# Sparse experts behind a shared one: a longer lag between the two products, weights in smaller parts, other orders of loads

## The chip, the cores and the metric
One NeuronCore of one Trainium2 chip. The metric is the device time of one execution in microseconds, median of the runs; lower is better. Everything is float32: each product of two float32 matrices is made of three matmuls, high x high, high x low and low x high, of the parts into which the operands are split.

## The reference, cut to what matters
x is [4, 1024, 512], so 4096 tokens of 512 features.

```
x = x + ((x * ys) @ weight) * d                         # modulated linear, ys and d from cond
s = sigmoid(concat(x, cond) @ router_W)                 # 8 experts
pick 2 experts of (s + router_bias) per token, gates = s_sel / sum(s_sel)
shared = (silu(x @ w1) * (x @ w3)) @ w2                 # 512 -> 1024 -> 512
routed = sum over the 2 experts: gate * (gelu(x @ W1e[e]) @ W2e[e])   # 512 -> 512 -> 512
out = x + (shared + routed) / 3
```

The router's weights are scaled up and its bias is drawn with a wide spread, so the load of the experts is uneven. From the inputs, 8192 (token, expert) rows fall on experts 4, 5, 6 and 7 alone: 3160, 622, 314 and 4096.

## The kernel before
Tokens go in 8 blocks of 512 (NBLK) through the linear layer and the router, then again in 8 blocks through the shared network, each in 8 chunks of 128 hidden features (HC): `up(n, hc, j)` is 24 matmuls, `down(n, hc)` 12. Meanwhile SP, ACT and DVE split the experts' weights into high and low parts, piece by piece (`move_piece`, `piece_high`, `piece_low`: load eraw, split into ehl, store to we_d), and POOL sorts the tokens by expert in memory: `put_row` scatters the rows of x1 with their token number and gate into xs_d.

Then come the experts. xs_d is cut into 71 tiles of 128 rows (TILES, the most that any routing needs), each of one expert; rows and tiles that the routing leaves empty are padding with gate 0 and a token number beyond the last token, one of 128 extra rows of out (PADROWS). Such rows are written by the loop at L1151. Per tile t:
- SP (pairs 0 and 1) or POOL (`load_pair`, L1170) loads x rows into xg, DVE turns them (`turn_x`), ACT and DVE split them (`x_high_of`, `take_x`).
- TensorE: `matmul1(t)`, 12 matmuls; ACT: gelu (`hidden`), and four DMAs hid to hturn (`move_h`, L676); DVE: `turn_h`; ACT, DVE: split (`h_high_of`, `take_h`).
- TensorE: `matmul2(t)`, 12 matmuls; DVE scales the result by the gate into ys (`take_y`, L1078); POOL adds it to the rows of out by an indirect DMA (`scatter`, L1184).

The loops run in a fixed order on each engine. TensorE's is matmul1(t), matmul2(t - LAG), with LAG = 3; ACT and DVE turn h of tile t - TURN_LAG, with TURN_LAG = 2. hid, hturn and ys have 4 buffers (RING), the split operands and the banks 2. So ys of tile t waits for the add of tile t - 4. An add waits for the one two tiles back; it also waits for the one just before unless both tiles are of one expert and neither is an unused tile (`scatter_waits` makes the table: `same`, `tail`).

Expert weights sit in four places (WRING) of 32 KB per partition, each in two halves, W1e and W2e, of 2 MB over all partitions. The used experts are numbered by turn. SP loads halves 0 to 7 for turns 0 to 3 first. Half 0 is loaded during block 6 of the shared network; half 1 waits for the last `up`, because place 0's second half and places 1 to 3 lie over w13h, w13l, the split w2 and xl. After that come the last store of out (`store_out(NBLK - 1)`, L282) and halves 2 to 7 (L328), each waited for before the next. Then, for rounds r = 4 to 7, SP reads a table, waits until TensorE has finished the tiles of turn r - 4 (L377; unused rounds all wait for the same tile, the last of turn 0) and loads two halves in four parts of 512 KB each (`load_in_parts`, L334), waiting for each part before it issues the next. This is done whether an expert is used or not. SP ends with waits for all stores and adds.

POOL, once the rows are sorted, waits for the scatter table and for the last store of out, then asks for pairs 2 and 3 of x, and then runs over the tiles: every second tile one more pair, and one scatter per tile.

Of the kernel before, what the change touches and what calls it, by code (L numbers as in the profile page):

```python
# [7 lines left out]
FP32 = mybir.dt.float32  # L8
FP32R = mybir.dt.float32r
INT32 = mybir.dt.int32  # L10
# [20 lines left out]
PAIR = 2  # L31
PADDED = -(-TILES // PAIR) * PAIR
SLOTS = PADDED * P
TURN_LAG = 2
LAG = TURN_LAG + 1
PADROWS = P
Q = 32
PADS = (SLOTS - K * TOK) // P
ROW = D + 2
XB = 4  # L40
EPS = 1e-8
# [24 lines left out]
def shared_moe_kernel(nc, xT, w0, condT, router_w, router_b, shared_w, expert_w, consts, tokid, padslots, padrows, out):  # L66
# [8 lines left out]
    with ctx:  # L75
        base = -(-nc.sbuf_base // 128) * 128

        def sb(name, shape, dt, kib):
            return nc.alloc_sbuf_tensor_at(name, [P] + shape, dt, offset=base + int(kib * KIB))

        def sem(name):
            return ctx.enter_context(nc.semaphore(name))


        x1t = sb("x1t", [2, DC, BLK], FP32, 0)
        w13h = sb("w13h", [HC, 2, DC, P], FP32R, 16)
        w13l = sb("w13l", [HC, 2, DC, P], FP32R, 48)
        wmh = sb("wmh", [2, DC, D], FP32R, 80)
        wml = sb("wml", [2, DC, D], FP32R, 96)
        w2h = wmh[:, :, :, :].rearrange("p b c n -> p (b c) n")  # L90
# [18 lines left out]
        xgt = sb("xgt", [2, DC, P], FP32, 192)  # L109
        wait_for = sb("wait_for", [TILES], INT32, 196)  # L110
        same = sb("same", [TILES], INT32, 196.5)
        tail = sb("tail", [TILES], INT32, 197)
        x1tok = sb("x1tok", [BLK // Q, DC, Q], FP32, 168)
        w0sq = sb("w0sq", [DC, D], FP32, 160)
        xres = sb("xres", [SUB, D], FP32, 160)
# [12 lines left out]
        def small(name, shape, dt=FP32):  # L128
            n = 1
            for s in shape:  # L130
                n *= s
            t = sb(name, shape, dt, at[0])
            at[0] += -(-n * 4 // 32) * 32 / KIB
            assert base + at[0] * KIB <= nc.sbuf_usable_end
            return t
# [15 lines left out]
        rec = small("rec", [K, NT, 2], INT32)  # L151
        sadr = small("sadr", [K, NT], INT32)
        padr = small("padr", [PADS], INT32)
        pad = small("pad", [3, 2 * E])
        slot = small("slot", [PADDED, 2], INT32)

# [57 lines left out]
        weights_in = sem("weights_in")  # L214
        xrow_in = [sem(f"xrow_in{b}") for b in range(XB)]
        xrow_out = [sem(f"xrow_out{b}") for b in range(XB)]
        rec_put, pad_done, zero_in, pad_out = sem("rec_put"), sem("pad_done"), sem("zero_in"), sem("pad_out")
        xg_in = [sem(f"xg_in{j}") for j in range(2)]
        xg_soft = [sem(f"xg_soft{j}") for j in range(2)]
        xturn_done, hturn_done, mm1_done, mm2_done = sem("xturn_done"), sem("hturn_done"), sem("mm1_done"), sem("mm2_done")  # L220
# [11 lines left out]
        def _(sp):  # L232
# [11 lines left out]
            sp.dma_start(xin[:, 1], xT[1]).then_inc(xin_in[1], 16)  # L244
            for j in range(2):
                sp.dma_start(wraw[:, j, :], shared_w[j]).then_inc(wraw_in[j], 16)
            sp.dma_start(out[TOK:TOK + PADROWS, :], padrows).then_inc(pads_in, 16)

            for n in range(NBLK):

# [57 lines left out]
            for n in range(NBLK - 2):  # L308
                for hc in range(HC):
                    if piece_at(n, hc):  # L310
                        move_piece(n, hc)
                    if n == 0 and hc == 1:
                        store_x1(0)
                    if n == 0 and hc == 2:
                        load_res(0)
                    if n and hc == 1:
                        store_out(n - 1)
                        load_res(n)
                    if hc == 5:
                        store_x1(n + 1)  # L320
                        load_x1t(n, n % 2)
# [4 lines left out]
            def load_weight(i, e, place):  # L326

                sp.dma_start(we[:, place, i % 2].rearrange("p a h s c n -> p (a h) (s c n)").bitcast(FP32),  # L328
                             we_d[bass.ds(e * 4 + i % 2 * 2, 2)].rearrange("h p s n -> p h (s n)").bitcast(FP32)).then_inc(we_in[i % HRING], 16)

            def load_in_parts(i, e, place):

                for q in range(4):
                    sp.dma_start(we[:, bass.ds(place, 1), i % 2, q // 2, q % 2].rearrange("p a c n -> p (a c n)").bitcast(FP32),  # L334
                                 we_d[bass.ds(e * 4 + i % 2 * 2 + q // 2, 1), :, q % 2].rearrange("a p n -> p (a n)").bitcast(FP32)).then_inc(we_in[i % HRING], 16)
                    sp.wait_ge(we_in[i % HRING], 16 + 16 * (q + 1))
                sp.sem_inc(weights_in, 1)

            def weight_loaded(i):
# [23 lines left out]
            for j in range(SUB):  # L363
                sp.dma_start(slot[j * Q:(j + 1) * Q], xs_rec[j]).then_inc(slots_in, 16)

            sp.wait_ge(ab_done, HC * NBLK)
            load_weight(1, first[0], slice(0, 1))
            store_out(NBLK - 1)
            weight_loaded(1)


            for i in range(2, HRING):
                load_weight(i, first[i // 2], slice(i // 2, i // 2 + 1))
                weight_loaded(i)
            for r in range(WRING, E):
                e, place, over = table(0, r, E - 1), table(1, r, WRING - 1), table(2, r, TILES)
                sp.wait_ge(mm2_done, over + 1)  # L377
                for i in (2 * r, 2 * r + 1):
                    load_in_parts(i, e, place)
            sp.wait_ge(pads_in, 16)  # L380
            sp.wait_ge(out_stored, 16 * NBLK)
            for j in range(2):
                sp.wait_ge(added[j], 16 * ((TILES - j + 1) // 2))
# [3 lines left out]
        def _(pe):  # L387
# [69 lines left out]
            def up(n, hc, j):  # L457

                q = HC * n + hc
                if hc == 0:  # L460
                    pe.wait_ge(xl_ready, 4 * (NBLK + n + 1))
                pe.wait_ge(gm_done, q + 1)
                for ps, m in ((a_ps, 0), (b_ps, 1)):
                    for c in range(DC):
                        w_hi, w_lo = w13h[:, hc, m, c, :], w13l[:, hc, m, c, :]
                        pe.matmul(ps[hc % 2][:, :], w_hi, xh[:, j, c, :], start=(c == 0), stop=False)  # L466
                        pe.matmul(ps[hc % 2][:, :], w_hi, xl[:, j, c, :], start=False, stop=False)  # L467
                        last = pe.matmul(ps[hc % 2][:, :], w_lo, xh[:, j, c, :], start=False, stop=(c == DC - 1))  # L468
                last.then_inc(ab_done, 1)
# [100 lines left out]
        def _(act):  # L570
# [13 lines left out]
            for n in range(NBLK):  # L584

                act.wait_ge(xin_in[(n + 1) % 2], 16 * ((n + 1) // 2) + 16)
                act.wait_ge(lin_done, DC * n + 1)
                for c in range(DC):
                    x_high((n + 1) % 2, c, mod[:, c, (n + 1) // 2:(n + 1) // 2 + 1] if n + 1 < NBLK else 1.0)
                if n == 0:  # L590
                    act.wait_ge(prep, 4)
                    act.activation(dtmp[:, :, :], dvar[:, :, :], ACT.Sqrt).then_inc(root, 1)

                act.wait_ge(wraw_in[n % 2], 16 * (n // 2) + 16)
                act.activation(w13h[:, n].rearrange("p m c n -> p (m c n)"), wraw[:, n % 2, :], ACT.Copy).then_inc(w_high, 1)

            def w2_high(g):

# [102 lines left out]
        def _(dve):  # L701
# [49 lines left out]
            for n in range(NBLK):  # L751
# [13 lines left out]
                        else:  # L765
                            x_low(n + 1, (n + 1) % 2, c)
                dve.wait_ge(w_high, n + 1)
                w_hi = w13h[:, n].rearrange("p m c n -> p (m c n)").bitcast(FP32)
                dve.tensor_tensor(w13l[:, n].rearrange("p m c n -> p (m c n)"), wraw[:, j, :], w_hi, ALU.subtract).then_inc(w_split, 1)

            def w2_low(g):
                dve.wait_ge(w_high, HC + g + 1)
# [130 lines left out]
            def pad_rows():  # L903
# [18 lines left out]
                then(dve.tensor_tensor(grid, grid, begin[:, 0:E + 1].unsqueeze(1).to_broadcast([P, PADS, E + 1]), ALU.mult))  # L922
                then(dve.tensor_reduce(dst[:, 0:PADS], grid, AX.X, ALU.max))
                then(dve.tensor_tensor(dst[:, 0:PADS], dst[:, 0:PADS], place, ALU.add))
                dve.tensor_copy(padr[:, :], dst[:, 0:PADS]).then_inc(pad_done, 1)

            def slot_rows():
# [151 lines left out]

            def scatter_waits():  # L1080

                at, used = cst[0:1, C_TIX:C_TIX + TILES], e8[0:1, 1, E - 1:E]
                then(dve.tensor_scalar(wait_for[0:1, :], at, 1.0, None, ALU.add))
                then(dve.tensor_scalar(wait_for[0:1, :], wait_for[0:1, :], 1, 255, ALU.logical_shift_right, ALU.bitwise_and))
                then(dve.tensor_tensor(same[0:1, 1:TILES], turn_of[0:1, 1:TILES], turn_of[0:1, 0:TILES - 1], ALU.is_equal))
                then(dve.tensor_scalar(tail[0:1, :], at, used, None, ALU.is_lt))
                then(dve.tensor_tensor(same[0:1, 1:TILES], same[0:1, 1:TILES], tail[0:1, 1:TILES], ALU.mult))
                then(dve.tensor_tensor(same[0:1, 1:TILES], wait_for[0:1, 1:TILES], same[0:1, 1:TILES], ALU.subtract))
                dve.tensor_scalar(wait_for[0:1, 1:TILES], same[0:1, 1:TILES], 16.0, None, ALU.mult).then_inc(waits_done, 1)

# [20 lines left out]
        def _(pool):  # L1111
# [28 lines left out]
            pool.wait_ge(tables_done, 3)  # L1140
            pool.wait_ge(sadr_done, K)
            pool.wait_ge(pad_done, 1)
            pool.dma_start(xrow[:, XB - 1, 0:D], padrows).then_inc(zero_in, 16)
            pool.dma_start(xrow[:, XB - 1, D:ROW].bitcast(INT32), padslots[:, 0:2]).then_inc(zero_in, 16)
            for i in range(XB - 1):
                load_row(i)
# [1 line left out]
            for g in range(PADS):  # L1148
                if g:
                    pool.wait_ge(pad_out, 16 * g)  # L1150
                pool.indirect_dma_start(xs_d[:, :], IO(padr[:, g:g + 1], 0), xrow[:, XB - 1, :], None).then_inc(pad_out, 16)  # L1151
            pool.wait_ge(pad_out, 16 * PADS)
            load_row(XB - 1)
            for i in range(0, NT, 2):
# [3 lines left out]
                for m in (i, i + 1):  # L1158
                    if m + XB < NT:
                        row_free(m)  # L1160
                        load_row(m + XB)
            pool.wait_ge(waits_done, 1)

            def load_pair(m):

# [18 lines left out]
                pool.indirect_dma_start(out[:, :], IO(slot[:, t, 0:1], 0), ys[:, t % RING, :], None,  # L1184
                                        compute_op=ALU.add).then_inc(added[t % 2], 16)

            pool.wait_ge(out_stored, 16 * NBLK)
            load_pair(2)
            load_pair(3)
            for t in range(TILES):  # L1190
                if t % 2 == 0:
                    load_pair(t // 2 + 4)
                scatter(t)
# [56 lines left out]
```

## Time and profile before
| | us |
|---|---|
| median of 3 runs (1078.06 to 1082.4) | 1079.09 |
| profiled execution, device time | 1082.94 |
| its span | 1081.1 |
| TensorE busy | 1030.0 |
| DVE busy | 507.4 |
| POOL busy | 332.3 |
| ACT busy | 292.7 |

The page's busy times are of the span of the profiled execution. The span falls into the linear layer (to about 116 us), the shared network (to about 647), and the experts. The engines' rows in the 40 slices show TensorE at 9 tenths or more in all but the first, one in the middle and the last few; the DMA engines' share is at 9 tenths or more in most slices of the experts' stage. A wait row names who ended the wait, by the last event that the profile shows.

### The profile page before, as it was taken

Reading aid. Unit: us, or ns where it says so; the run is one execution under the profiler, and the core shown is the slowest. Engines: PE = TensorE matmul, PEld = TensorE weight load, DVE = VectorE, ACT = ScalarE, POOL = GpSimd, SP = SyncE. Lnnn points to the kernel's source line nnn. Section 1 sums busy time; section 2 is a strip of 40 time slices with the busy share of each in tenths; the row PEclk is TensorE's granted clock in tenths of the full one; section 3 lists DMA queues with packets and bytes.
Section 4 is the critical chain, followed back from the end, with each engine's and each line's share of the span. In section 5 each row is a group of like instructions: output and inputs, shape, how many; then the busy total and the mean of one; then the engine's idle time right before and its main releaser. Section 6 shows DMA issues by size and latency. Waiting matters only on the chain.

```text
span 1081.1 us, 14559 instructions
## 1 busy us (share of the span) xinstructions
PE 1030.0 (95%) x4692; PEld 841.7 (78%) x4692; DVE 507.4 (47%) x829; ACT 292.7 (27%) x461; POOL 332.3 (31%) x385
## 2 busy tenths in 40 slices
PE   6999999999999999999999995989999999999993
PEld 5888778887888888888888883878888887878782
DVE  4565456577324324324232123555555555555452
ACT  3222252332222222222111122223333333233230
POOL 1000000001113424334324102445545555555532
PEclk9999999999999999999999998999999999999997
DMA  5566587768867676877735629997779999999963
GB/s 177 195 216 228 205 285 258 243 242 237 280 217 263 209 271 225 244 276 238 235 96 155 134 78 282 294 266 136 155 135 197 238 200 230 219 223 213 210 126 56
DMA packets 132026, 226.77 MB, mean 210 GB/s; under 512 B 28848, under 2 KB 83760, under 8 KB 122864
## 3 DMA queue, kind: packets, MB, share of 16 engines
q1 hardware_dynamic: 59168, 142.22, 40.9%
q0 software_dynamic: 31328, 64.11, 26.2%
q10 hardware_dynamic: 41472, 19.68, 8.2%
q8 instruction: 35, 0.57, 0.2%
q14 instruction: 23, 0.19, 0.1%
HBM read 111.01 MB, written 96.54 MB: 192 GB/s over the span
## 4 chain that ended last, share of the span: by engine, by line
PE 75%; DMA 16%; DVE 3%; issue 3%; ACT 1%; SPq 1%; POOLq 0%; POOL 0%; DVEq 0%
DMA we<-we_d 12%; PE banks L466 10%; PE banks L467 10%; PE banks L468 10%; PE banks L528 7%; PE banks L530 7%; PE banks L529 7%; PE banks L480 5%; PE banks L481 5%; PE banks L482 5%; DMA out<-ys,slot 4%; PE banks L414 3%; PE banks L415 3%; PE banks L416 3%; PE banks L446 1%
## 5 line engine op out<-in xcount | busy, mean ns | idle before, releaser
L466 PE MATMUL banks<-xh,w13h 128*128 128x512 f32 x512 | 200.1, 391 | 1.8 <-DVE xl L723 1.8
L468 PE MATMUL banks<-xh,w13l 128*128 128x512 f32 x512 | 199.9, 390 | 0.0
L467 PE MATMUL banks<-xl,w13h 128*128 128x512 f32 x512 | 199.9, 390 | 0.0
L1184 POOL DMA_INDIRECT out<-ys,slot x71 | 123.9, 1745 | 202.5 <-DMA out<-ys,slot 118.8
L791 DVE SCALAR_TENSOR_TENSOR gm<-sil,banks 128x512 f32<-128x512 f32 x64 | 43.9, 687 | 248.2 <-ACT sil L609 248.2
L528 PE MATMUL banks<-we,hidth 128*128 x284 | 114.3, 402 | 16.2 <-issue 15.2
L1071 DVE TENSOR_TENSOR hidtl<-hidt,hidth 128x512 fp32r<-128x512 f32 x71 | 49.2, 693 | 161.6 <-ACT hidth L683 161.6
L609 ACT ACTIVATE sil<-banks 128x512 f32<-128x512 f32 x64 | 38.3, 598 | 314.8 <-PE banks L468 314.8
L1170 POOL DMA_DIRECT2D xg<-xs_d x136 | 99.9, 1113 | 63.1 <-DMA out<-outst 51.0
L528 PE MATMUL banks<-we,xgth 128*128 x284 | 111.4, 392 | 5.0 <-issue 4.4
L466 PEld LDWEIGHTS banks<-xh,w13h 128*128 128x128 f32 x512 | 96.7, 189 | 22.4 <-issue 2.3
L530 PE MATMUL banks<-we,hidtl 128*128 x284 | 112.4, 396 | 0.0
L529 PE MATMUL banks<-we,hidth 128*128 x284 | 112.2, 395 | 0.0
L468 PEld LDWEIGHTS banks<-xh,w13l 128*128 128x128 f32 x512 | 96.5, 188 | 20.2
L467 PEld LDWEIGHTS banks<-xl,w13h 128*128 128x128 f32 x512 | 96.5, 188 | 19.9
L529 PE MATMUL banks<-we,xgth 128*128 x284 | 110.6, 389 | 0.0
L530 PE MATMUL banks<-we,xgtl 128*128 x284 | 110.5, 389 | 0.0
L683 ACT ACTIVATE hidth<-hidt 128x512 fp32r<-128x512 f32 x71 | 44.9, 633 | 215.3 <-PE banks L530 126.7
L480 PE MATMUL banks<-wmh,gh 128*128 128x512 f32 x256 | 100.5, 392 | 2.5 <-DVE gl L795 1.9
L481 PE MATMUL banks<-wml,gh 128*128 128x512 f32 x256 | 100.4, 392 | 0.0
L482 PE MATMUL banks<-wmh,gl 128*128 128x512 f32 x256 | 100.3, 392 | 0.0
L528 PEld LDWEIGHTS banks<-we,hidth 128*128 128x128 f32 x284 | 54.1, 190 | 35.1 <-issue 24.2
(163 smaller groups left out, 1465.0 us busy)
## 6 DMA issues: line engine op xcount, KB each, us to landing
we_d<-ehl SPq DMA_DIRECT2D x32, 1024.0 KB, 6.4
hturn<-hid ACTq DMA_DIRECT2D x284, 64.0 KB
xg<-xs_d POOLq DMA_DIRECT2D x136, 128.0 KB
eraw<-expert_w SPq DMA_DIRECT2D x32, 512.0 KB, 5.0
we<-we_d SPq DMA_DIRECT2D x8, 2048.0 KB, 10.3
we<-we_d SPq DMA_DIRECT2D x32, 512.0 KB, 6.2
x1t_d<-x1t SPq DMA_DIRECT2D x8, 1024.0 KB, 8.6
xin<-x1t_d SPq DMA_DIRECT2D x8, 1024.0 KB, 9.4
```

Source lines behind the costliest of these rows:

```text
L466: pe.matmul(ps[hc % 2][:, :], w_hi, xh[:, j, c, :], start=(c == 0), stop=False)
L467: pe.matmul(ps[hc % 2][:, :], w_hi, xl[:, j, c, :], start=False, stop=False)
L468: last = pe.matmul(ps[hc % 2][:, :], w_lo, xh[:, j, c, :], start=False, stop=(c == DC - 1))
L480: pe.matmul(o_ps[s][:, :], g_hi, w2h[:, hc, :], start=(hc == 0), stop=False)
L481: pe.matmul(o_ps[s][:, :], g_hi, w2l[:, hc, :], start=False, stop=False)
L482: last = pe.matmul(o_ps[s][:, :], g_lo, w2h[:, hc, :], start=False, stop=(hc == HC - 1))
L528: pe.matmul(ps, high[:, c, :], w_hi, start=(c == 0), stop=False)
L529: pe.matmul(ps, high[:, c, :], w_lo, start=False, stop=False)
L530: last = pe.matmul(ps, low[:, c, :], w_hi, start=False, stop=(c == DC - 1))
L1071: dve.tensor_tensor(hidtl[:, t % 2], hidt[:, t % 2], hidth[:, t % 2].bitcast(FP32), ALU.subtract).then_inc(hidt_done, 1)
L1170: pool.dma_start(xg[g * Q:(g + 1) * Q, m % 2 * PAIR:(m % 2 + 1) * PAIR].rearrange("p t a n -> p (t a) n"), xs_d[m * PAIR * P:(m + 1) * PAI ...
L1184: pool.indirect_dma_start(out[:, :], IO(slot[:, t, 0:1], 0), ys[:, t % RING, :], None, compute_op=ALU.add).then_inc(added[t % 2], 16)
```

## The change: lag, parts, order of loads, padding
- TURN_LAG 3 and LAG 4, so matmul2 runs four tiles behind matmul1.
- w13h and w13l become one tensor w13 with high and low parts of a chunk side by side, so that 16 KB become free with every two chunks. Halves 1 to 3 of the experts' weights wait for `ab_done` of the last block's chunks (2, 4 and 6 done), not for the whole block.
- Half 4 waits for the last `up` and is loaded in parts, then `store_out(NBLK - 1)` is issued, and then halves 5 to 7, also in parts. A part is 256 KB, 8 to a half, in rows of 2 KB, each waited for before the next.
- POOL asks for pairs 2 and 3 of x before it waits for the last store of out.
- Padding rows have their own row of out, 8 x 128 of them (PADROWS); POOL writes the token numbers of each pad group by one more copy. The zeros for them (2 MB) are stored in block 1 of the shared network instead of 256 KB at the start. Unused tiles of one turn no longer wait for the add just before (`tail` goes).

```
-TURN_LAG = 2
+TURN_LAG = 3
 LAG = TURN_LAG + 1
-PADROWS = P
+PADROWS = PADS * P
...
-        w13h = sb("w13h", [HC, 2, DC, P], FP32R, 16)
-        w13l = sb("w13l", [HC, 2, DC, P], FP32R, 48)
+        w13 = sb("w13", [HC, 2, 2 * DC * P], FP32R, 16)
...
-            sp.dma_start(out[TOK:TOK + PADROWS, :], padrows).then_inc(pads_in, 16)
...
+                    if n == 1 and hc == 3:
+                        sp.dma_start(out[TOK:TOK + PADROWS, :], padrows).then_inc(pads_in, 16)
...
+            parts_before = [16 if i < 4 else 0 for i in range(HRING)]
+
             def load_in_parts(i, e, place):
 
-                for q in range(4):
-                    sp.dma_start(we[:, bass.ds(place, 1), i % 2, q // 2, q % 2].rearrange("p a c n -> p (a c n)").bitcast(FP32),
-                                 we_d[bass.ds(e * 4 + i % 2 * 2 + q // 2, 1), :, q % 2].rearrange("a p n -> p (a n)").bitcast(FP32)).then_inc(we_in[i % HRING], 16)
-                    sp.wait_ge(we_in[i % HRING], 16 + 16 * (q + 1))
+                for q in range(8):
+                    half, part, c = q // 4, q // 2 % 2, q % 2
+                    sp.dma_start(we[:, place, i % 2, half, part, c].rearrange("p a n -> p (a n)").bitcast(FP32),
+                                 we_d[bass.ds(e * 4 + i % 2 * 2 + half, 1), :, part, c * D:(c + 1) * D].rearrange("a p n -> p (a n)").bitcast(FP32)).then_inc(we_in[i], 16)
+                    sp.wait_ge(we_in[i], parts_before[i] + 16 * (q + 1))
+                parts_before[i] += 128
                 sp.sem_inc(weights_in, 1)
...
-            sp.wait_ge(ab_done, HC * NBLK)
-            load_weight(1, first[0], slice(0, 1))
-            store_out(NBLK - 1)
-            weight_loaded(1)
-
-
-            for i in range(2, HRING):
+            for i in (1, 2, 3):
+                sp.wait_ge(ab_done, HC * (NBLK - 1) + 2 * i)
                 load_weight(i, first[i // 2], slice(i // 2, i // 2 + 1))
                 weight_loaded(i)
+            sp.wait_ge(ab_done, HC * NBLK)
+            load_in_parts(4, first[2], slice(2, 3))
+            store_out(NBLK - 1)
+            for i in range(5, HRING):
+                load_in_parts(i, first[i // 2], slice(i // 2, i // 2 + 1))
             for r in range(WRING, E):
                 e, place, over = table(0, r, E - 1), table(1, r, WRING - 1), table(2, r, TILES)
                 sp.wait_ge(mm2_done, over + 1)
                 for i in (2 * r, 2 * r + 1):
-                    load_in_parts(i, e, place)
-            sp.wait_ge(pads_in, 16)
+                    load_in_parts(i % HRING, e, bass.ds(place, 1))
...
+                then(dve.tensor_scalar(padtok[:, :], tid[:, 0:PADS], float(TOK), None, ALU.add))
...
-                then(dve.tensor_scalar(tail[0:1, :], at, used, None, ALU.is_lt))
-                then(dve.tensor_tensor(same[0:1, 1:TILES], same[0:1, 1:TILES], tail[0:1, 1:TILES], ALU.mult))
...
+                pool.tensor_copy(xrow[:, XB - 1, D:D + 1].bitcast(INT32), padtok[:, g:g + 1]).then_inc(pad_put, 1)
+                pool.wait_ge(pad_put, g + 1)
                 pool.indirect_dma_start(xs_d[:, :], IO(padr[:, g:g + 1], 0), xrow[:, XB - 1, :], None).then_inc(pad_out, 16)
...
-            pool.wait_ge(waits_done, 1)
...
-            pool.wait_ge(out_stored, 16 * NBLK)
             load_pair(2)
             load_pair(3)
+            pool.wait_ge(waits_done, 1)
+            pool.wait_ge(pads_in, 16)
+            pool.wait_ge(out_stored, 16 * NBLK)
```

## Rows read from the trace of the kernel before
**Rows 1.** The page, part 1: busy us (share of span) x instructions.
```profile
PE 1030.0 (95%) x4692; PEld 841.7 (78%) x4692; DVE 507.4 (47%) x829; ACT 292.7 (27%) x461; POOL 332.3 (31%) x385
```
**Rows 2.** Windows of 5 us: us, busy by engine, granted clock, DMA share, GB/s.
```profile
670.00:675.00 5.00, 4.20 (x10) 3.33 (x11) 2.88 (x5) 2.00 (x4) 2.30 (x4) 0.50 1.03 351
```
**Rows 3.** TensorE's timeline: start us, us, engine, line, what [idle before <-releaser].
```profile
646.88 0.39 PE L528 MATMUL banks<-we,xgth 128*128 x1
...
660.86 0.49 PE L528 MATMUL banks<-we,xgth 128*128 x1 [1.68 <-issue]
...
670.80 0.79 PE L528 MATMUL banks<-we,hidth 128*128 x1 [6.39 <-issue]
...
962.79 0.39 PE L528 MATMUL banks<-we,xgth 128*128 x1
...
968.23 0.39 PE L528 MATMUL banks<-we,xgth 128*128 x1
```
**Rows 4.** Timelines of DVE, ACT's queue and POOL, 640 to 740 us.
```profile
665.38 0.71 DVE L1052 STREAM_TRANSPOSE xgt<-xg 128x512 f32<-128x512 f32 x1 [4.72 <-DMA xg<-xs_d]
668.50 0.71 DVE L1065 STREAM_TRANSPOSE hidt<-hturn 128x512 f32<-128x512 f32 x1 [2.42 <-DMA hturn<-hid]
...
650.48 3.53 ACTq L676 DMA_DIRECT2D hturn<-hid  x4
...
655.38 4.70 POOL L1170 DMA_DIRECT2D xg<-xs_d  x8 [50.96 <-DMA out<-outst]
```
**Rows 5.** Timelines of DVE and POOL at the end.
```profile
1065.68 0.75 DVE L1078 TENSOR_SCALAR ys<-banks,slot 128x512 f32<-128x512 f32 x1 [2.52 <-PE banks L530]
...
1047.29 1.55 POOL L1184 DMA_INDIRECT out<-ys,slot  x1 [4.17 <-DMA out<-ys,slot]
...
1075.77 1.55 POOL L1184 DMA_INDIRECT out<-ys,slot  x1 [4.50 <-issue]
```
**Rows 6.** SP's timeline from 540 us: start, us from first to last issue, what.
```profile
610.97 5.81 SPq L364 DMA_DIRECT2D slot<-xs_d  x4
641.38 0.42 SPq L328 DMA_DIRECT2D we<-we_d  x1
649.59 0.40 SPq L282 DMA_DIRECT2D out<-outst  x1
...
812.16 211.97 SPq L334 DMA_DIRECT2D we<-we_d  x32
```
**Rows 7.** POOL: a copy of its timeline, and a wait (us, times, longest).
```profile
602.63 0.54 POOL L1129 COPY xrow<-rec 128x2 int32<-128x2 int32 x1
...
POOL xrow L1119 <- DMA x_d<-x1tok: 17.5, 1, 17.5
```
**Rows 8.** Timelines of SP and ACT in block 1 of the shared network.
```profile
230.53 0.33 SPq L304 DMA_DIRECT2D eraw<-expert_w  x1
...
240.57 0.60 ACT L609 ACTIVATE sil<-banks 128x512 f32<-128x512 f32 x1 [5.23 <-PE banks L468]
```
**Rows 9.** Landing times of L328 (2048 KB), then of L334 (512 KB).
```profile
DMA to landing us min/median/max: 7.7/10.3/13.8
...
DMA to landing us min/median/max: 4.5/6.2/9.8
```
**Rows 10.** SP's waits, 812 to 1024 us: us, times, longest.
```profile
SPq L334 <- DMA we<-we_d: 142.6, 24, 9.2
...
SPq L337 <- DMA we<-we_d: 45.3, 7, 9.4
```
**Rows 11.** Landing of other DMAs: 200 to 500 us; SP's loads of xg.
```profile
x_d<-x1tok SPq DMA_DIRECT2D x19, 256.0 KB, 5.8
...
xg<-xs_d SPq DMA_DIRECT2D x8, 128.0 KB, 3.2
```
**Rows 12.** DMA queues, 812 to 1024 us: packets, MB, share of 16 engines.
```profile
q0 software_dynamic: 9111, 19.92, 48.4%
...
q10 hardware_dynamic: 21590, 9.83, 21.5%
```

More of the change, by code:

```diff
@@ L111, in shared_moe_kernel @@
         same = sb("same", [TILES], INT32, 196.5)
-        tail = sb("tail", [TILES], INT32, 197)
         x1tok = sb("x1tok", [BLK // Q, DC, Q], FP32, 168)
@@ L153, in shared_moe_kernel @@
         padr = small("padr", [PADS], INT32)
+        padtok = small("padtok", [PADS], INT32)
         pad = small("pad", [3, 2 * E])
@@ L216, in shared_moe_kernel @@
         xrow_out = [sem(f"xrow_out{b}") for b in range(XB)]
-        rec_put, pad_done, zero_in, pad_out = sem("rec_put"), sem("pad_done"), sem("zero_in"), sem("pad_out")
+        rec_put, pad_put, pad_done, zero_in, pad_out = sem("rec_put"), sem("pad_put"), sem("pad_done"), sem("zero_in"), sem("pad_out")
         xg_in = [sem(f"xg_in{j}") for j in range(2)]
@@ L464, in up @@
                     for c in range(DC):
-                        w_hi, w_lo = w13h[:, hc, m, c, :], w13l[:, hc, m, c, :]
+                        w_hi, w_lo = (w13[:, hc, k, (m * DC + c) * P:(m * DC + c + 1) * P] for k in range(2))
                         pe.matmul(ps[hc % 2][:, :], w_hi, xh[:, j, c, :], start=(c == 0), stop=False)
@@ L594, in _ @@
                 act.wait_ge(wraw_in[n % 2], 16 * (n // 2) + 16)
-                act.activation(w13h[:, n].rearrange("p m c n -> p (m c n)"), wraw[:, n % 2, :], ACT.Copy).then_inc(w_high, 1)
+                act.activation(w13[:, n, 0, :], wraw[:, n % 2, :], ACT.Copy).then_inc(w_high, 1)
             def w2_high(g):
@@ L767, in _ @@
                 dve.wait_ge(w_high, n + 1)
-                w_hi = w13h[:, n].rearrange("p m c n -> p (m c n)").bitcast(FP32)
-                dve.tensor_tensor(w13l[:, n].rearrange("p m c n -> p (m c n)"), wraw[:, j, :], w_hi, ALU.subtract).then_inc(w_split, 1)
+                dve.tensor_tensor(w13[:, n, 1, :], wraw[:, j, :], w13[:, n, 0, :].bitcast(FP32), ALU.subtract).then_inc(w_split, 1)
             def w2_low(g):
@@ L1080, in scatter_waits @@
             def scatter_waits():
-                at, used = cst[0:1, C_TIX:C_TIX + TILES], e8[0:1, 1, E - 1:E]
-                then(dve.tensor_scalar(wait_for[0:1, :], at, 1.0, None, ALU.add))
+                then(dve.tensor_scalar(wait_for[0:1, :], cst[0:1, C_TIX:C_TIX + TILES], 1.0, None, ALU.add))
                 then(dve.tensor_scalar(wait_for[0:1, :], wait_for[0:1, :], 1, 255, ALU.logical_shift_right, ALU.bitwise_and))
                 then(dve.tensor_tensor(same[0:1, 1:TILES], turn_of[0:1, 1:TILES], turn_of[0:1, 0:TILES - 1], ALU.is_equal))
-                then(dve.tensor_scalar(tail[0:1, :], at, used, None, ALU.is_lt))
-                then(dve.tensor_tensor(same[0:1, 1:TILES], same[0:1, 1:TILES], tail[0:1, 1:TILES], ALU.mult))
                 then(dve.tensor_tensor(same[0:1, 1:TILES], wait_for[0:1, 1:TILES], same[0:1, 1:TILES], ALU.subtract))
@@ L1142, in _ @@
             pool.wait_ge(pad_done, 1)
-            pool.dma_start(xrow[:, XB - 1, 0:D], padrows).then_inc(zero_in, 16)
+            pool.dma_start(xrow[:, XB - 1, 0:D], padrows[0:P]).then_inc(zero_in, 16)
             pool.dma_start(xrow[:, XB - 1, D:ROW].bitcast(INT32), padslots[:, 0:2]).then_inc(zero_in, 16)
```

## The prediction
> **What bounds the kernel now.** I read the page first: TensorE is busy 95% of the span [rows 1], so two questions follow: where it stands still, and what comes after its last instruction. The windows of 5 us put one weak place in front: 670 to 675 runs at a granted clock of 0.50, so at 1.2 GHz and not 2.4, with 10 matmuls [rows 2]. TensorE's timeline gives the pace of the expert stage: two first products in succession start at 962.79 and 968.23, so a tile (two products of 12 matmuls) costs 5.44 us, a product 2.72. There are 71 tiles, 142 products, 386 us of work. The first starts at 646.88; the first second product starts at 670.80 after 6.39 us of idle time [rows 3]. DVE shows why: its turn of x waits 4.72 us for a transfer that POOL issued only at 655.38, after 50.96 us of waiting for the last store of out, and its turn of h waits another 2.42 us for a move issued from 650.48 on, beside 2 MB weight loads [rows 4].
>
> At the end, the last scaling of a result starts at 1065.68, but the last scatter-add is issued at 1075.77; the one of tile 65 went at 1047.29 [rows 5]. That is five steps of 5.70 us, each waiting for the one before to land. The reason is in the routing: worked out from the reference's inputs, only experts 4, 5, 6 and 7 are chosen, for 3160, 622, 314 and 4096 rows, that is 25 + 5 + 3 + 32 = 65 tiles; tiles 65 to 70 are padding and write the same rows.
>
> SP is the third thing to read, though nobody waits for it late. Its timeline has one merged row of 32 reload parts from 812.16 on, 211.97 us long [rows 6]. Rounds 4 to 7 ask for experts that were not chosen: nobody uses them, but the program can't end before SP has waited for the last part. Before, SP was through near 1030 (812.16 + 211.97 and a landing) and then waited for the scatters.
>
> **The parts of the change that save.** *Padding.* With own rows, tiles 65 to 70 may have two adds in flight. The last add then follows the last scaling: 1075.77 - (1065.68 + 0.75 + about 0.2) = 9 us less. Cost: 8 copies on POOL of 0.54 us and some 0.3 us of wait each, 7 us near 300 us; POOL later waits 17.5 us for the last block of x1 [rows 7], so nothing is left of it (7 us if that cover is gone, and even then the 24 us between SP's last slot load and 641.38 hide it [rows 6]). The zero store grows to 2 MB and moves behind piece 11, near 225. The next piece load was issued at 230.53, and would queue behind it by up to 10 us; ACT stands idle 5.23 us before 240.57 waiting for TensorE [rows 8], and TensorE itself has another 5 us or so. I take 0, with 0 to 5 as bounds. The copy of indices on DVE against two small operations removed there: 0.
>
> *Weights 1, 2, 3.* SP finishes the slot loads near 616.8 (610.97 + 5.81) and could issue half 1 then, not at 641.38 [rows 6]; chunks of w13 are free two by two. Landing takes 7.7 to 10.3 us [rows 9], so halves 1 to 3 are in near 643. The layout of w13 alone changes no operand's size: 0.
>
> *x sooner.* Pair 2 is asked for when tiles 0 and 1 are turned, near 645, not at 655.38: the 4.72 us wait goes.
>
> *Lag of four.* Five first products now stand before the first second product. In this start ACT sets the pace, not TensorE: one gelu of 0.6, four moves of 2.5 to 3.5 us together [rows 4] and one copy of 0.63, some 4.5 us a tile. Counting on from first product 3 at 660.86 [rows 3], product 4 starts near 664.6, and the first second product near 668.6 once ACT has issued the moves of tile 3. That is 2.2 us sooner with one product more done, so 4.9 us; half speed up to 676.7 would cost another 3 us and may come anyway, the gaps before being the same. Later TensorE stops (8 us between 670.80 and 812.16: 141.4 less 24 x 5.44 + 2.72 and the slow stretch counted in) mostly go, since h has 5.44 us more to arrive. The drain has four second products instead of three at much the same 3 us: 0.
>
> TensorE would then end near 668.6 + 137 x 2.72 = 1041, plus 5 us for the waits of the drain and of the clock: 1047. With 0.75 for the scaling and some 5.5 for the last add: 1053, so 28 us less. This holds if nothing else ends later.
>
> **The part that costs: 256 KB parts, one at a time.** SP waits for each part before it issues the next. The 32 parts of 512 KB had a pitch of 211.6 / 31 = 6.83 us; the waits after issue, 142.6 over 24 and 45.3 over 7 [rows 10], with some 0.4 for the issue (0.42 at 641.38, rows 6) give a landing of 6.4, and the rest is 0.15 a part and 8 us for register loads in all. Now the same bytes are 64 parts, and before them halves 4 to 7 are 32 parts more.
>
> What does a part of 256 KB take? The trace has no such reload, so from both sides. Medians first: 2048 KB takes 10.3 and 512 KB 6.2 [rows 9]: 2.7 us per MB, so a quarter MB less saves 0.7 and leaves 5.7. Minima: 7.7 and 4.5, so 4.0 for 256 KB. If the whole crowded share scales with bytes: quiet 3.4 plus half of the other 3.0 is 4.9. Stores of 256 KB from SP in the shared stage took 5.8 at the median, 128 KB loads with nothing beside them 3.2 [rows 11]. In the reload window POOL's queue alone takes 48.4% of the engines' time and ACT's 21.5% [rows 12], which does not change. I take 5.0, nearest the 4.9 since half of SP's own bytes per second goes too; ends 4.0 and 5.8. After TensorE's end, with quiet queues, 3.5.
>
> The Trainium skill ("DMA: Bandwidth & Descriptors", section on the anatomy of one DMA) gives 2.0 us plus bytes over 436 GB/s for a DMA of POOL's path. By that rule 512 KB would be 3.2 us, where rows 9 show 6.2, and 256 KB 2.6. It is a rival below. The same page (queues, rings and completion order) says that each DMA engine serves its queues in turn, packet by packet; halving the size of packets would then not shorten the waits between them, and the part would be nearer 5.7. The rows decide neither.
>
> The sum. Half 4 starts at 643 and takes 8 parts in light traffic, near 4.2 each: 677. Then the last store of out goes, 27 us later than at 649.59 [rows 6]; POOL's pair 4 and first scatter wait for it until about 683, when first product 8 needs x near 688: an even race, 0 to 8 us. Halves 5 to 7: 24 x 5.15 and 2 = 126: 803. Second product 24 is done at 668.6 + 24 x 5.44 + 2.72 = 802. So the reload starts at 804. Up to 1047, (243 - 7) / 5.15 = 46 parts; the other 18 at 3.65 are 66 us. SP ends at 1113, the span at about 1115. Every saving above is hidden behind it. At 5.8 the end is 1136; at 4.0 it is 1073. TensorE sets the end only if a part takes no more than (1053 - 811) / 64 = 3.8 all told.
>
> The profiled execution of before took 1082.94 us, 1.8 over its span, and lay 3.85 over the median of 1079.09. So 1115 + 1.8 - 3.85 = 1113.
>
> **Rivals.**
> 1. *The parts are quick and stay hidden* (faster). For it: nothing in the old trace waits for a reload, the 128 KB loads took 3.2, and SP had 50 us to spare. Against it: one at a time, twice as many, and 4.5 is the least that 512 KB took in 32 tries. Time: 1053 - 2 = 1051; with the slow clock in front or the late store of out, up to 1062. This is what the skill's fixed cost plus bytes would give. Chance 0.17.
> 2. *Parts near 4.2*: 236 / 4.35 = 54 by 1047, 10 left, 37 us: 1084 and no difference, within 0.5% of 1079 (what a measurement of this kernel tells from no change), or somewhat below. Chance 0.11, of which 0.05 is faster.
> 3. *The late store of out starves the start*: if the parts of half 4 take 5.15, the store goes at 684 and x of tiles 8 and 9 comes at 695 against 688. TensorE stands some 8 us and may lose clock as well; second product 24 is late by as much, and so is the reload behind it: 1113 + 8 = 1121. For it: SP's order in the code. Against: light traffic then. Chance 0.15.
> 4. Forecast as summed, 1113: 0.57.
>
> **How the numbers follow.** The likeliest is the forecast: 1113, of its own 1092 to 1136. Slower by over 0.5%: 0.57 + 0.15 = 0.72. Same: 0.06. Faster: 0.17 + 0.05 = 0.22. For 8 in 10 the range reaches from 1062 (rival 1 at its slow end, parts at 3.8 to 4) to 1136 (parts at 5.8).
>
> **What would show it.** Right: SP's row of reload parts has 64 issues, starts near 804 and runs past 1090, TensorE's last matmul lies near 1047, and the chain of waits ends in loads of we. Scatter-adds of tiles 65 to 70 are about 3 us apart, not 5.7. The idle 6.39 us before the first second product is gone, and the last store of out is issued after the 8 parts of half 4. Wrong: a median landing under 4 us, or SP through before 1050; then the time is near 1051. Also wrong if TensorE stands still over 10 us between 680 and 800.

## The result, and the profile after

The changed kernel takes 1112.49 us in the median of 4 runs (1107.66 to 1116.59), against 1080.17 for the kernel before, measured beside it: a ratio of 1.0297, 95% interval 1.0249 to 1.0346. The forecast was 1113. The span of its profiled execution is 1111.8.

SP's timeline of the changed kernel answers to [rows 6]: start, us from first to last issue, what.

```profile
609.31 6.12 SPq L368 DMA_DIRECT2D slot<-xs_d  x4
615.64 17.16 SPq L328 DMA_DIRECT2D we<-we_d  x3
640.21 27.20 SPq L337 DMA_DIRECT2D we<-we_d  x8
670.25 0.39 SPq L280 DMA_DIRECT2D out<-outst  x1
670.85 437.66 SPq L337 DMA_DIRECT2D we<-we_d  x88
```

Halves 1 to 3 went in three loads from 615.64, half 4 in 8 parts from 640.21, and only then the last store of out, at 670.25, 20.7 us later than in the kernel before. The last row is the answer to the whole change: 88 parts, 24 of halves 5 to 7 and 64 of the reload, the last issued near 1108.5. The same view in three stretches shows the reload's start and the two paces:

```profile
804.76 0.36 SPq L337 DMA_DIRECT2D we<-we_d  x1
...
812.45 238.26 SPq L337 DMA_DIRECT2D we<-we_d  x46
...
1054.33 54.18 SPq L337 DMA_DIRECT2D we<-we_d  x17
```

One, 46 and 17 parts are the 64 of the reload. From 804.76 to 1054.33 there are 47 steps of 5.31 us, while TensorE, ACT and POOL are at work; from then on 16 steps of (54.18 - 0.36) / 16 = 3.36. SP's waits in the stretches 803 to 1052 and 1052 to 1112 (us, times, longest) say what fills them:

```profile
SPq L337 <- DMA we<-we_d: 174.6, 38, 8.3
SPq L341 <- DMA we<-we_d: 31.0, 5, 8.1
...
SPq L337 <- DMA we<-we_d: 40.6, 15, 3.4
SPq L341 <- DMA we<-we_d: 9.1, 3, 3.5
```

That is 205.6 / 43 = 4.78 us of waiting for a part in the crowded stretch and 49.7 / 18 = 2.76 in the quiet one; with the issue of 0.36, landings of 5.1 and 3.1. The view gives no landing times for this line; in experiment 3, where it gives them for 15 parts in quiet queues, their median is 3.0.

TensorE's timeline (start, us, what, idle before) answers to [rows 3]:

```profile
666.13 0.49 PE L531 MATMUL banks<-we,hidth 128*128 x1 [0.22 <-issue]
...
685.25 0.50 PE L531 MATMUL banks<-we,hidth 128*128 x1 [2.52 <-issue]
...
1039.57 0.49 PE L531 MATMUL banks<-we,hidth 128*128 x1 [2.16 <-issue]
...
1051.07 0.39 PE L533 MATMUL banks<-we,hidtl 128*128 x1
```

The idle 6.39 us before the first second product have become 0.22, although five first products stand ahead of it now. TensorE ends at 1051.46, where it ended at 1065.64 before. The windows of the changed kernel (us, busy by engine, granted clock, DMA share, GB/s) show one weak place near 685, with a granted clock of 0.66, and then nothing for the last 60 us:

```profile
680.00:685.00 5.00, 2.73 (x13) 1.92 (x11) 1.95 (x4) 1.30 (x3) 0.83 (x2) 1.00 0.87 181
685.00:690.00 5.00, 4.75 (x14) 3.77 (x15) 3.32 (x7) 1.48 (x3) 3.24 (x5) 0.66 0.71 142
...
1040.00:1111.00 71.00, 11.24 (x48) 8.38 (x46) 6.97 (x11) 1.90 (x3) 7.76 (x5) 0.61 0.40 94
```

DVE's and POOL's rows explain the place near 685: the turn of x waits for a load that POOL could issue only after the store of out, the order that the third rival named.

```profile
682.36 0.71 DVE L1055 STREAM_TRANSPOSE xgt<-xg 128x512 f32<-128x512 f32 x1 [4.59 <-DMA xg<-xs_d]
...
675.71 2.31 POOL L1171 DMA_DIRECT2D xg<-xs_d  x4 [18.63 <-DMA out<-outst]
```

POOL's last adds answer to [rows 5]. The last four are 3.0 to 4.2 us apart instead of 5.70, and the last is issued 58 us before the end:

```profile
1043.63 1.55 POOL L1185 DMA_INDIRECT out<-ys,slot  x1 [1.78 <-DVE ys L1081]
1046.65 1.55 POOL L1185 DMA_INDIRECT out<-ys,slot  x1 [1.46 <-DVE ys L1081]
1049.70 1.55 POOL L1185 DMA_INDIRECT out<-ys,slot  x1 [1.50 <-DVE ys L1081]
1053.85 1.55 POOL L1185 DMA_INDIRECT out<-ys,slot  x1 [2.60 <-issue]
```

So TensorE ends 14 us sooner than before and the last add goes 22 us sooner, and all of that lies in front of SP's last 17 parts. Which part of the change saved it is a question for the experiments; the lag did not.

### The profile page after: what moved, and what is told of

Same layout as the page of the kernel before. It is cut to its first block, busy times and chain, and to the rows that moved or that the text cites. A ratio compares the mean times of both kernels' runs of the same rounds, so it can differ in the third digit from the quotient of the medians.

```text
span 1111.8 us, 14746 instructions
## 1 busy us (share of the span) xinstructions
PE 1025.2 (92%) x4692; PEld 838.8 (75%) x4692; DVE 506.3 (46%) x828; ACT 292.8 (26%) x461; POOL 335.7 (30%) x393
## 4 chain that ended last, share of the span: by engine, by line
PE 79%; DMA 8%; DVE 4%; issue 2%; SPq 1%; ACT 1%; POOLq 0%; DVEq 0%
PE banks L531 12%; PE banks L533 12%; PE banks L532 11%; PE banks L469 8%; PE banks L471 8%; PE banks L470 8%; DMA we_d<-ehl 5%; PE banks L483 4%; PE banks L485 4%; PE banks L484 4%; PE banks L417 3%; PE banks L418 3%; PE banks L419 3%; DMA eraw<-expert_w 1%; PE banks L449 1%
## 5 line engine op out<-in xcount | busy, mean ns | idle before, releaser
L469 PE MATMUL banks<-xh,w 128*128 128x512 f32 x512 | 200.3, 391 | 1.8 <-DVE xl L726 1.8
L471 PE MATMUL banks<-xh,w 128*128 128x512 f32 x512 | 199.8, 390 | 0.0
L470 PE MATMUL banks<-xl,w 128*128 128x512 f32 x512 | 199.7, 390 | 0.0
L531 PE MATMUL banks<-we,hidth 128*128 x284 | 112.5, 396 | 7.5 <-issue 7.5
L469 PEld LDWEIGHTS banks<-xh,w 128*128 128x128 f32 x512 | 96.5, 188 | 22.2 <-issue 2.3
L470 PEld LDWEIGHTS banks<-xl,w 128*128 128x128 f32 x512 | 96.5, 189 | 20.2
L471 PEld LDWEIGHTS banks<-xh,w 128*128 128x128 f32 x512 | 96.5, 188 | 20.1
L532 PE MATMUL banks<-we,hidth 128*128 x284 | 111.3, 392 | 0.0
```

The costliest lines, as they stand in the source:

```text
L531: pe.matmul(ps, high[:, c, :], w_hi, start=(c == 0), stop=False)
L532: pe.matmul(ps, high[:, c, :], w_lo, start=False, stop=False)
```

## The experiments

All ratios are to the kernel before on the chip of that set, with a 95% interval.

**1. The changed kernel without the reload.** Rounds 4 to 7 are left out; these inputs use none of what they load, others would.

```
-            for r in range(WRING, E):
+            for r in range(0):
```

> The changed kernel without rounds 4 to 7 of the weight loads, which no tile of these inputs uses (other inputs would need them). Theory (SP's 64 serial parts set the end): TensorE's last matmul stays near 1050, the last add lands near 1059, time 1056 us, 56 under the changed kernel. Rival (another part of the change, the longer lag or the late store of out, costs the 30 us): the time stays over 1090.

Measured: 1062.24 us (1061.8 to 1065.14), ratio 0.9865 (0.9821 to 0.991). Without the reload the changed kernel is some 50 us faster, and faster than the kernel before. It came 6 over what I expected (1056 could not stand beside a last add that lands near 1059, as I had it): TensorE's first second product starts at 668.03 here, and its last matmul at 1052.43.

**2. The changed kernel with the reload in parts of 512 KB.**

```
-                    load_in_parts(i % HRING, e, bass.ds(place, 1))
+                    load_wide(i % HRING, e, bass.ds(place, 1))     # 4 parts, as before
```

> The changed kernel with the reloads in four parts of 512 KB again; halves 4 to 7 stay in parts of 256 KB. Theory: 32 parts of 6.83 us from 805 end near 1025, hidden behind TensorE, so 1057 us, as without reloads. Rival (what costs is that the same 16 MB are read at all, or where the reload starts, and not the size of a part): over 1090. If contention of larger parts counts, TensorE's stops grow by some us over the kernel without reloads: 1060 to 1065.

Measured: 1066.04 us (1059.94 to 1069.85), ratio 0.9879 (0.982 to 0.9938). The same 16 MB from the same start are hidden. The row of SP's timeline, and behind it the landing line of L346:

```profile
808.83 206.44 SPq L346 DMA_DIRECT2D we<-we_d  x32
```

```profile
DMA to landing us min/median/max: 4.5/5.7/7.5
```

31 steps of 6.65 us for 512 KB, against 5.31 for 256 KB: half the bytes saved 20% of the time. The time is 9 us over what I expected for hidden reloads. The profiled execution has a stop of TensorE of 5.46 us before 688.59, a longer form of the 2.52 us of the changed kernel, while DVE waits 7.35 us for x (until 685.70); the granted clock is 0.81 and 0.84 in the two windows of 5 us from 685 on.

**3. The kernel before with parts of 256 KB.**

```
-                for q in range(4):
+                for q in range(8):
+                    half, part, c = q // 4, q // 2 % 2, q % 2
...              # one part of 256 KB per DMA, each waited for
```

> The kernel before with one edit: reloads in eight parts of 256 KB. Theory: the reload starts at 812, 48 parts of some 5 us are done when TensorE ends near 1062, the other 16 take 3.2 each, so SP ends near 1114 and the time is about 1114 us, 34 over before. Rival (SP has room in the old order, parts shrink with their bytes): 1080, no change.

Measured: 1119.07 us (1115.97 to 1122.13), ratio 1.0383 (1.0332 to 1.0434). One edit of one loop makes all of the loss, and more, since nothing else is gained. SP's timeline, and then its waits from 1062 on (us, times, longest):

```profile
813.38 300.89 SPq L335 DMA_DIRECT2D we<-we_d  x64
```

```profile
SPq L335 <- DMA we<-we_d: 38.9, 14, 3.5
SPq L338 <- DMA we<-we_d: 8.4, 3, 3.3
```

The time is 5 us over what I expected: up to 1058.37 there are 47 steps of 5.21 us, not 5.0, and the 16 quiet steps behind are 3.47, not 3.2. The waits in the quiet stretch are 47.3 / 17 = 2.8.

**4. The kernel before with the padding part alone.**

```
-PADROWS = P
+PADROWS = PADS * P
-                then(dve.tensor_scalar(tail[0:1, :], at, used, None, ALU.is_lt))
-                then(dve.tensor_tensor(same[0:1, 1:TILES], same[0:1, 1:TILES], tail[0:1, 1:TILES], ALU.mult))
...              # and the store of zeros in block 1, POOL's copy per pad group
```

> The kernel before with the padding part of the change alone (own rows of out for every pad, unused tiles' adds overlap, zeros of 2 MB stored in block 1). Theory: the last six adds stop being 5.70 us apart and follow the last scaling at 1065.7, so 9 us less: 1071 us; the 2 MB store and POOL's copies cost nothing. Rival (the adds are bound by their landing in POOL's queue whatever rows they write): 1080. Rival (the 2 MB store delays the expert pieces and TensorE stands still in block 1): 1073 to 1078.

Measured: 1071.5 us (1067.0 to 1078.11), ratio 0.9939 (0.9906 to 0.9972), so 6.6 us less with 3 to 10 as bounds. The rival of no change is out; the rival of 1073 to 1078 is not out by the time alone, but by TensorE, which shows no stop where it put one. DVE's last scaling and POOL's last adds (timelines):

```profile
1060.76 0.75 DVE L1079 TENSOR_SCALAR ys<-banks,slot 128x512 f32<-128x512 f32 x1 [2.54 <-PE banks L530]
...
1055.77 1.55 POOL L1185 DMA_INDIRECT out<-ys,slot  x1 [3.40 <-DMA out<-ys,slot]
1058.49 1.55 POOL L1185 DMA_INDIRECT out<-ys,slot  x1 [1.17 <-DVE ys L1079]
1062.22 1.55 POOL L1185 DMA_INDIRECT out<-ys,slot  x1 [2.18 <-DVE ys L1079]
```

The last add is issued 0.7 us after the scaling ends, where it was 9.3 after. The 2 MB store was issued at 222.17; TensorE has no stop from 200 to 263, and then one of 0.74 us that the kernel before has too (0.52).

**5. The store of out first.** Experiment 2 with these two lines exchanged:

```
+            store_out(NBLK - 1)
             load_in_parts(4, first[2], slice(2, 3))
-            store_out(NBLK - 1)
```

> The changed kernel with reloads in parts of 512 KB, as in the run before, and the last store of out issued ahead of the parts of half 4 instead of behind them. Theory: x of tiles 8 and 9 waits for that store through POOL's order, which is the 5.46 us stop and the half clock at 683 to 695 of the run before; with the store at 648 it goes: 6 to 8 us less than 1066, so 1059. Rival (the stop comes from POOL's turn or ACT and not from the store): 1066 again.

Measured: 1063.35 us (1060.55 to 1067.63), ratio 0.9835 (0.9801 to 0.987); experiment 2 had 0.9879. The stop of 5.46 us is gone from the profile (TensorE has no stop over 0.4 us between 670 and 790), and DVE waits for no x there. The time falls by 3 us by the medians and 5 by the ratios, less than the 6 to 8 expected, and the two intervals overlap. In this profiled execution the expert stage also began 2 us later, so the stop's cause is shown, and its price only as small.

**6. Two parts in flight.** The changed kernel with parts of 256 KB, but SP waits for the part before the last.

```
+        part_in = [sem(f"part_in{j}") for j in range(2)]
...
-                                 ...).then_inc(we_in[i], 16)
-                    sp.wait_ge(we_in[i], parts_before[i] + 16 * (q + 1))
+                                 ...).then_inc(part_in[parts[0] % 2], 16)
+                    parts[0] += 1
+                    if q:
+                        sp.wait_ge(part_in[parts[0] % 2], 16 * (parts[0] // 2))
+                sp.wait_ge(part_in[(parts[0] - 1) % 2], 16 * ((parts[0] + 1) // 2))
```

> The changed kernel with its parts of 256 KB, but SP waits for the part before the last, so two are in flight (within a half). Theory (the price is the latency of each part in series, not the bytes or the number of DMAs): some 3 us a part where it was 4.9, so the reload ends near 1000 and the time is TensorE's, 1062 to 1066 us. Rival (the queues are full and a part lands later by as much as it is issued sooner): the reload still runs past 1090, time over 1095.

Measured: 1060.07 us (1059.69 to 1061.88), ratio 0.9818 (0.979 to 0.9845): 52 us under the changed kernel with the same bytes in the same 96 DMAs. SP's timeline, and then its waits from 800 on:

```profile
640.68 14.35 SPq L340 DMA_DIRECT2D we<-we_d  x8
661.48 354.06 SPq L340 DMA_DIRECT2D we<-we_d  x88
...
803.51 212.03 SPq L340 DMA_DIRECT2D we<-we_d  x63
```

```profile
SPq L340 <- PE banks L538: 62.0, 1, 62.0
SPq L391 <- DMA out<-ys,slot: 34.6, 1, 34.6
```

Half 4 took 14.35 us instead of 27.20. The halves were in so early that SP waited 62 us for the last tile of turn 0, and at the end another 34.6 us for the adds. The third row is the reload but for its first issue: 62 steps of (212.03 - 0.44) / 62 = 3.41 us, with TensorE, ACT and POOL at work, where the serial parts took 5.31. The windows of the two reloads (the changed kernel first) and then SP's own queue (packets, MB, share of 16 engines) in the changed kernel from 804 to 1050, in this one from 804 to 1015, and in the kernel before from 812 to 1024:

```profile
804.00:1052.00 248.00, 242.70 (x1059) 197.52 (x1057) 139.28 (x219) 75.36 (x129) 130.04 (x126) 1.00 0.91 186
804.00:1015.00 211.00, 208.68 (x912) 170.16 (x911) 120.85 (x190) 65.79 (x114) 114.10 (x115) 1.00 1.00 220
...
q1 hardware_dynamic: 6624, 12.06, 19.9%
q1 hardware_dynamic: 8928, 16.26, 31.5%
q1 hardware_dynamic: 4464, 16.25, 28.6%
```

A part is 144 packets at either size in the profile's count, for 6624 packets are 46 parts of 256 KB and 4464 are 31 of 512 KB. Its packets took 0.199 x 246 / 46 = 1.06 us of the 16 engines with 256 KB and 0.286 x 212 / 31 = 1.96 with 512 KB. So the engines' work on a part did halve, nearly, and was small beside the step of 5.31; for the rest of it SP waited with this one part on its queue. What cost the 32 us was the latency of one part after the other, not the number of parts and not the engines' work on shorter rows. With two in flight the DMA engines' share is at 1.00, so three or more may gain nothing in the crowd; that was not tried.

**7. The changed kernel without the reload and with the old lag.** TURN_LAG 2, second products three tiles behind.

> The changed kernel without rounds 4 to 7 of the loads and with the old lag (TURN_LAG 2, second product three tiles behind). Theory (the longer lag gives the moved h 5.44 us more and one more first product at the start, worth 5 us in front and some later stops): 1062 + 6 = 1068 us. Rival (once weights and x come in time the lag is worth nothing): 1062.

Measured: 1058.07 us (1055.83 to 1063.07), ratio 0.9805 (0.9765 to 0.9844), against 0.9865 (0.9821 to 0.991) with the lag of four. My theory wanted 6 us more than experiment 1 and got 4 us less by the medians, 6 by the ratios, with intervals that just overlap. The first second product starts sooner, at 662.62, after 1.06 us of idle time, with four first products ahead of it and not five:

```profile
662.62 0.50 PE L531 MATMUL banks<-we,hidth 128*128 x1 [1.06 <-issue]
```

**8. The kernel before with the longer lag alone.** TURN_LAG 3.

> The kernel before with TURN_LAG 3 alone. Theory: TensorE gains up to 5 us in front and up to 8 in stops behind, but adds of the unused tiles stay in series, so about 1080 - 8 = 1072 us; if x of tile 4, still late, sets the start, only 4 us: 1076. Rival: 1080, the lag does nothing where POOL's adds set the pace of the end.

Measured: 1082.51 us (1080.77 to 1085.22), ratio 1.0019 (1.0002 to 1.0036): nothing gained. The stop of 6.39 us before the first second product goes, but one of 3.49 appears at 667.63 ahead of first product 4, and two more later. DVE turns x before it turns h, and x is what comes late:

```profile
665.26 0.71 DVE L1052 STREAM_TRANSPOSE xgt<-xg 128x512 f32<-128x512 f32 x1 [4.86 <-DMA xg<-xs_d]
...
701.05 0.71 DVE L1052 STREAM_TRANSPOSE xgt<-xg 128x512 f32<-128x512 f32 x1 [5.27 <-DMA xg<-xs_d]
...
715.42 0.71 DVE L1052 STREAM_TRANSPOSE xgt<-xg 128x512 f32<-128x512 f32 x1 [5.65 <-DMA xg<-xs_d]
```

In the kernel before, DVE waited for h at these places:

```profile
712.23 0.71 DVE L1065 STREAM_TRANSPOSE hidt<-hturn 128x512 f32<-128x512 f32 x1 [3.86 <-DMA hturn<-hid]
...
724.37 0.71 DVE L1065 STREAM_TRANSPOSE hidt<-hturn 128x512 f32<-128x512 f32 x1 [3.80 <-DMA hturn<-hid]
```

So the longer lag did take away the waits for h that it was meant for, but x was late as well, and the wait for x took their place. Why the x of 701 and 715 comes late no run isolates.

**9 to 11. The best of it, with and without lag and order.** Experiment 6 with the store of out first; the same with a lag of three; experiment 6 with a lag of three alone. All three ran on one chip.

> The kernel with two parts in flight, and the last store of out ahead of half 4 as well; second products four tiles behind. If the late store costs anything where half 4 is through by 661: up to 3 us less than 1060, so 1057. If it does not (the parts are quick enough): 1060.

> The same with second products three tiles behind (TURN_LAG 2). Theory after the last runs (with weights and x in time, h has arrived after two tiles, so the longer lag only adds a product of prologue at ACT's pace): 1055, 1 to 4 us less than with the lag of four on this chip. Rival (my first theory, the lag covers h's move): 3 to 5 us more.

> Two parts in flight, lag of three tiles, the store of out behind half 4 as in the change. Expected 1057: against the kernel with the lag of four and otherwise the same (1060.07 in the last set) it shows the lag alone once more; against the one with the store first, the store alone.

| | us (lowest to highest) | ratio, 95% interval |
|---|---|---|
| store first, lag 4 | 1060.33 (1055.26 to 1062.58) | 0.9819 (0.9788 to 0.9851) |
| store first, lag 3 | 1056.51 (1054.18 to 1062.98) | 0.9796 (0.976 to 0.9832) |
| store behind half 4, lag 3 | 1057.81 (1055.3 to 1062.07) | 0.979 (0.9759 to 0.982) |

Two parts in flight and a lag of three make the version that beats both kernels, about 2% under the kernel before and 5% under the changed one. It loads all that the changed kernel loads, so by its code it serves other routings too; only these inputs were run. The medians of the lag of three lie 2.5 to 4 us below the lag of four, as in experiment 7, but the intervals overlap. The order of the store is worth nothing measurable once half 4 is through by 661: 1056.51 against 1057.81 with the lag of three, 1060.33 against 1060.07 (experiment 6) with that of four.

## Why the prediction was right, step by step

*What sets the end.* Right: SP's serial parts. Experiments 1, 2 and 6 take away the reload, its small parts and the serial wait in turn, and the loss goes each time; experiment 3 takes away all of the change but the small parts, and the loss stays.

*A part of 256 KB.* Taken as 5.0 us crowded and 3.5 quiet, measured 5.1 and 3.1. The ends 4.0 and 5.8 held it. The steps were 5.31 and 3.36, where the sum had 5.15 plus 7 us in all, and 3.65. By the minima alone, 4.0, the change would have been faster; the working that halves the crowd's share, 4.9, came nearest. Its inputs are weaker than its result: no row shows the quiet 3.4, and the reason that half of SP's own bytes per second goes was not borne out (12.06 MB in 246 us against 16.25 in 212, so 49 GB/s against 77). The working by medians has a slip: 6.2 - 0.7 is 5.5; 5.7 comes out of the mean of 6.4. So the size of a part was a choice among 4.0, 4.9 and 5.7 that the rows of the kernel before could not make. The Trainium skill's 2.0 us plus bytes over 436 GB/s, for a DMA of POOL's path ("DMA: Bandwidth & Descriptors", anatomy of one DMA), gives an estimate of 2.6 us: no run here shows so little for the serial parts, 3.1 in quiet and 5.1 in a crowd. By the Trainium skill's rule that an engine takes the queues in turn by packets (same page, queues, rings and completion order) the waits stay as they are when packets are halved. In the profile's count a part is 144 packets at either size, and the landing falls from 6.4 to 5.1, by 1.3 us, of which 0.9 are the engines' own work (1.96 less 1.06, experiment 6); the other 0.4 and the waits themselves no run takes apart, so the runs don't decide it.

*The start of the reload.* 804 forecast, 804.76 measured. 46 parts by 1047 were forecast; 47 steps ended at 1054.33.

*The span and the time.* The span was forecast at 1115 and was 1111.8: one part more went at the crowded pace (some 2 us), the quiet ones were 5 us quicker in all, and next to nothing follows SP's last landing, where I had 2 us. The conversion was off the other way: the profiled execution of before happened to lie 3.85 us over its median, and I carried this over; that of the changed kernel lies about 1 us over. The two errors of 3 us cancel, so the half a microsecond between 1113 and 1112.49 is luck; some 3 us is what the sum was good for.

*TensorE's end.* 1047 forecast, 1051.5 measured. The first second product came 2.5 us sooner than taken (666.13, not 668.6), but the waits behind it were mis-sized: 1051.5 - (666.13 + 137 x 2.72) = 12.7 us instead of 5. The stops in the rows are 2.52 near 685, 2.16 in the drain and 2.6 in several of up to 0.8, together 7.3, and the clock of 0.66 over 5 us is worth 1.7; the other 4 us I have not traced. This is why experiment 1 stayed at 1062, and it would have made rival 1's time 1051 too small by 10.

*The lag.* Wrong as a saving. I gave it 4.9 us in front and most of 8 us behind. Experiments 7 and 8 give it nothing, and perhaps a loss of a few us. The start's gain is not the lag's: with the old lag the first second product comes at 662.62, 8.2 us sooner than in the kernel before, so by exclusion it belongs to x and the weights asked for sooner, which I had given no price of their own. The waits for h behind it were real in the kernel before (3.86 and 3.80 us), but with the longer lag alone x held DVE at the same places (experiment 8), and with the rest of the change but the reload DVE waits for no h even at the old lag (experiment 7). Together the parts other than padding and lag are worth some 8 to 14 us (experiments 1 and 7, less the 6.6 of padding); no run takes x sooner and weights sooner apart.

*Padding.* 9 us forecast, 6.6 measured (3 to 10); adds as expected. The 2 MB store and POOL's copies show no cost: TensorE has no stop behind the store, and SP's slot loads, which come after POOL's sorting, start at 609.31 against 610.97.

*The late store of out.* It happened, at 670.25 and not 677, for half 4 took (27.20 - 0.36) / 7 = 3.8 us a part, not 4.2, and began 3 us sooner. Its stop was 2.52 us and a short stretch at the lower clock, hidden behind SP in the changed kernel; up to 5.46 in experiment 2.

*What would show it.* The signs of being right came but for one, and those of being wrong did not: SP ran to 1108.5, and TensorE's longest stop between 680 and 800 was 2.52 us. The sign that failed was badly chosen: the chain of waits of the changed kernel does not end in loads of we. Its last pieces are those of the adds:

```profile
1046.65 4.98 DMA out<-ys,slot
1052.35 1.27 issue
1053.62 1.77 POOLq L75
```

It stops 56 us before the span does. The part of SP that only waits and issues is not in the chain; SP's timeline shows it.

## What to carry to other kernels

Before transfers are cut into smaller ones, count how many then stand in series on their queue, multiply by the landing in the crowded stretch, and compare with the slack of that queue; a serial DMA of half the size can cost far more than half, here 80% of the step. If small parts are wanted for the sake of other traffic, keep two in flight: here that brought the step from 5.31 to 3.41. And look at work that nobody waits for: a queue that loads unused data is harmless only until it is the last to finish.

## What the runs showed that I had not expected

Serial loads of 256 KB step at 3.36 us with quiet queues and at 5.31 with POOL's and ACT's queues at work; loads of 512 KB at 6.65 to 6.83 in the same crowd. The slope between the two crowded steps is 1.3 to 1.5 us per 256 KB, and 3.8 to 4 us a step don't shrink with the size. Two in flight make the crowded step 3.41, as short as a serial one in quiet queues, although the DMA engines' share already stood at 0.91 with one in flight. A high share of busy engines did not mean that nothing was to be gained: it rose to 1.00, and the bytes moved from 186 to 220 GB/s. A part waited for latency far more than for the engines' work on it, 1.06 us of its 5.31.
